# A decoder's second cross-attention: the order of the work behind its last item, and the banks that this work uses

## The chip, the core and the metric

The program runs on one core of one Trainium2 chip. A core has TensorE (PE: matmuls and transpositions, results to eight banks of PSUM), VectorE (DVE), ScalarE (ACT), GpSimd (POOL) and SyncE (SP), each with an instruction stream of its own, which runs in order; they wait for each other through semaphores. The metric is device time in microseconds for one execution, from the launch to the end of the last store. Smaller is better.

## What is computed

Two decoder layers; each is an attention, a cross-attention and a feed-forward part, with x = layernorm(x + part(x)) behind each. x is 8 items of 112 tokens by 256 values, the context 8 items of 375 by 192. The change lies in the second layer's cross-attention, whose stage also holds the last feed-forward part:

```python
def _L1_xattn_ref(x, context, Wq, Wk, Wv, Wo, bo):      # 8 heads of 128
    q = (x @ Wq).reshape(B, Tq, h, C) * SCALE
    k = (context @ Wk).reshape(B, Tk, h, C) * SCALE
    v = (context @ Wv).reshape(B, Tk, h, C)
    attn = jax.nn.softmax(jnp.einsum('bqhc,bkhc->bhqk', q, k), axis=-1)
    out = jnp.einsum('bhqk,bkhc->bqhc', attn, v).reshape(B, Tq, h * C)
    return out @ Wo + bo

def _L1_ffn_ref(x, base_w, base_b, lora_A, lora_B, router_w, router_b):
    result = jnp.einsum('bsd,od->bso', x, base_w) + base_b
    logits = jnp.einsum('bsd,ed->bse', x, router_w) + router_b
    gating = jax.nn.softmax(logits, axis=-1).astype(jnp.bfloat16)
    mid = jnp.einsum('bsd,dr->bsr', x, lora_A)
    lora_out = jnp.einsum('bsr,erd,bse->bsd', mid, lora_B, gating.astype(jnp.float32))
    return result + lora_out * SCALING
```

## The kernel before

The stages follow each other on the core: a state-space part, a cross-attention, a mixture of experts, a latent attention, and last `wide_cross_attention`, from about 727 us to the end of the profile. There the key and value weights are folded into the query and output weights, so scores are taken with the context itself, and the weighted context goes through `w_b`.

**Items and strips.** The loop runs over items i = 0 to 7 and over four strips u = 0 to 3 of two heads each. For a strip TensorE makes the scores of the next strip (`scores`, banks 1 and 2) and transposes the probabilities of this one (`turn`, banks 3 and 4). VectorE takes the maxima (`row_max`), copies the turned probabilities to SBUF (`copy_turned`) and scales the next ones (`normalize_heads`); ScalarE takes the exponentials (`exps`). For two strips, a half of an item, `weigh(i, half)` multiplies the turned probabilities with the context into banks 5, 6 and 7, called U_BANK: twelve matmul records for the first two, twelve for bank 7. `collect(i, half)` brings them back in two halves: ScalarE casts three tiles to fp32r (`ot_high`), VectorE subtracts the rest (`ot_low`). A `weigh` waits for the copies of its strips and for the `collect` before it. Half 1 of an item is weighed in the next item's strip 0; that of item 7 has no such place and stands behind the loop.

**Jobs.** All else of TensorE's work is a list of jobs with a number each: QUERY (queries of two items), CTX_REST and CTX_MAIN (transposing the context), OUT (output weights, 36 matmuls in fp32r), NT (transposing the normalized item), BASE (the feed-forward part's dense product with router and low-rank input), GATES (transposing the gated low-rank values) and LOW (their product with `lora_b`). `jobs(i, u, at)` says which job stands where in a strip (EARLY, MID, LATE), and `first_left` and `left` those behind the loop. All go through bank 0 (`JOB`): a job waits until `job_used` has counted every job before it, that is, until ScalarE (`drain`: QUERY, CTX, GATES, NT) or VectorE (`residual` for OUT, `base` for BASE, `add_low` for LOW) has emptied the bank. OUT also waits for both halves of `collect`, NT for `normalize`, GATES for `gates`.

**One item's way after its attention:** OUT, `residual` (add, statistics), `deviation` (ScalarE), `normalize`, NT, its copy to `xt`, BASE, `base` (small part, add, maximum), `gate_exps` (ScalarE), `gates`, GATES, its copy to `gm_t`, LOW, `add_low` (add, statistics), `end_deviation` (ScalarE), `finish`, store of the item by SyncE in the items' order. So several items are under way when the loop ends. Ahead of NT (7), TensorE runs eight products of the identity (`stream`), whose result nobody reads.

The order on each engine is the order in which these calls are written out. Line 1355 and 1358 are the scores, 1367 the turnings, 1382 the weighing's part in bank 7, 1306 and 1309 the context, 1319 GATES, 1321 LOW, 1324 NT; matmuls of line 101 are QUERY, OUT, BASE or weighing, told apart by their tiles.

## Time and profile before

| | us |
|---|---|
| timed runs, median of 3 | 997.63 (996.88 to 999.98) |
| profiled execution | 994.54 |
| its span, first to last instruction or packet | 992.7 |
| PE busy | 953.7 (96% of the span) |
| DVE busy | 587.3 (59%) |
| ACT busy | 414.3 (42%) |

A busy PE isn't PE at its peak, since matmuls are pipelined. The page's 40 slices show PE at nine or more tenths nearly throughout, and at 7 and 5 in the last two; the clock's row reads 9 (full) in all but the last, which reads 8. The chain that ended last consists of PE at the greatest part of its shares. Views used below are the timeline (instructions by start, merged, with the idle time of the engine before them), the chain, and tables of stretches with the granted clock, where 1.00 is the full 2.4 GHz and 0.50 is 1.2 GHz. A chain's piece lasts until the next one takes over, so it can be shorter than the same instruction in the timeline.

### The profile page before, as it was taken

Reading aid. Unit: us, or ns where it says so; the run is one execution under the profiler, and the core shown is the slowest. Engines: PE = TensorE matmul, PEld = TensorE weight load, DVE = VectorE, ACT = ScalarE, POOL = GpSimd, SP = SyncE. Lnnn points to the kernel's source line nnn. Section 1 sums busy time; section 2 is a strip of 40 time slices with the busy share of each in tenths; the row PEclk is TensorE's granted clock in tenths of the full one; section 3 lists DMA queues with packets and bytes.
Section 4 is the critical chain, followed back from the end, with each engine's and each line's share of the span. In section 5 each row is a group of like instructions: output and inputs, shape, how many; then the busy total and the mean of one; then the engine's idle time right before and its main releaser. Section 6 shows DMA issues by size and latency. Waiting matters only on the chain. (4 is left out here: it accounts for less than half of the span.)

```text
span 992.7 us, 17284 instructions
## 1 busy us (share of the span) xinstructions
PE 953.7 (96%) x6584; PEld 744.9 (75%) x6584; DVE 587.3 (59%) x1342; ACT 414.3 (42%) x1088; POOL 154.3 (16%) x151
## 2 busy tenths in 40 slices
PE   9899899999999999989999999999989999999975
PEld 4687777877878777768999998666657777767653
DVE  3788645555555565657756565368646454565554
ACT  3556534343343333436454545367643233232321
POOL 0333620110110100004443442300010000000000
PEclk9999999999999999999999999999999999999998
DMA  5500010000000000008511100720000000000000
GB/s 161 206 1 1 10 60 1 17 17 1 16 2 1 1 2 1 1 2 291 163 43 42 43 1 10 171 38 2 2 19 16 17 16 17 16 1 25 6 6 18
DMA packets 26825, 36.34 MB, mean 37 GB/s; under 512 B 3648, under 2 KB 22160, under 8 KB 26752
## 3 DMA queue, kind: packets, MB, share of 16 engines
q1 hardware_dynamic: 26752, 35.35, 12.1%
q8 instruction: 48, 0.79, 0.3%
q14 instruction: 25, 0.20, 0.1%
HBM read 30.75 MB, written 2.75 MB: 34 GB/s over the span
## 5 line engine op out<-in xcount | busy, mean ns | idle before, releaser
L1164 ACT ACTIVATE x_prob<-bank,x_negmax 112x375 f32<-112x375 f32 x128 | 72.2, 569 | 143.9 <-DVE x_negmax L1072 143.9
L1912 DVE TENSOR_TENSOR moe_h_low<-moe_sq,moe_h_high 128x512 fp32r<-128x512 f32 (+1 forms) x64 | 54.4, 871 | 50.6 <-ACT moe_h_high L2012 38.0
L1989 POOL TENSOR_TENSOR moe_sq<-moe_r 128x512 f32<-128x512 f32 (+1 forms) x64 | 64.2, 1006 | 102.8 <-ACT moe_r L2021 81.0
L1072 DVE TENSOR_REDUCE x_negmax<-bank 112x1 f32<-112x375 f32 x128 | 64.1, 542 | 9.5 <-PE bank L956 7.3
L2021 ACT ACTIVATE moe_r<-bank 128x512 f32<-128x512 f32 (+1 forms) x64 | 34.9, 545 | 72.6 <-PE bank L101 68.7
L101 PE MATMUL bank<-moe_w_low,moe_h_high 128*128 128x256 f32 x224 | 63.3, 283 | 0.0
L101 PE MATMUL bank<-moe_w_high,moe_h_low 128*128 128x256 f32 x224 | 63.3, 283 | 0.0
L101 PE MATMUL bank<-moe_w_high,moe_h_high 128*128 128x256 f32 x224 | 63.3, 283 | 0.0
L1077 DVE COPY x_prob_t<-bank 125x336 f32<-125x336 f32 x128 | 58.4, 497 | 2.9 <-PE bank L965 1.4
L956 PE MATMUL bank<-x_kt,x_qt 64*112 64x375 f32 x256 | 58.3, 521 | 1.2 <-issue 0.7
L1595 ACT ACTIVATE x_prob<-bank,x_negmax 112x375 f32<-112x375 f32 x64 | 36.1, 568 | 45.8 <-DVE x_negmax L1448 45.8
L965 PEld LDWEIGHTS bank<-const,x_prob 112*125 112x125 f32 x384 | 49.9, 188 | 6.6 <-issue 3.8
L965 PE MATMUL bank<-const,x_prob 112*125 112x112 f32 x384 | 52.8, 273 | 0.9 <-DVE x_prob_t L1077 0.8
L977 PEld LDWEIGHTS bank<-x_prob_t,x_v 125*64 125x64 f32 x768 | 37.0, 136 | 19.0 <-issue 15.2
L925 POOL COPY x_inv<-x_inv_head 112x512 f32<-112x512 f32 x16 | 9.8, 614 | 265.2 <-DVE x_inv_head L1083 265.2
L1604 ACT CAST x_ot_high<-bank 128x224 fp32r<-128x224 f32 x48 | 13.5, 354 | 81.9 <-PE bank L101 50.6
L977 PE MATMUL bank<-x_prob_t,x_v 125*64 125x112 f32 x768 | 45.4, 264 | 0.0
L101 PE MATMUL bank<-moe_xt_high,moe_w_high 128*128 128x384 f32 (+1 forms) x120 | 44.1, 367 | 1.0 <-DVE moe_w_low L1918 0.9
L1064 DVE COPY x_v<-bank 125x512 f32<-125x512 f32 x24 | 16.6, 691 | 45.4 <-PE bank L101 45.4
L101 PE MATMUL bank<-moe_xt_high,moe_w_low 128*128 128x384 f32 (+1 forms) x120 | 43.2, 360 | 0.0
L101 PE MATMUL bank<-moe_xt_low,moe_w_high 128*128 128x384 f32 (+1 forms) x120 | 43.2, 360 | 0.0
L101 PEld LDWEIGHTS bank<-moe_w_low,moe_h_high 128*128 128x128 f32 x224 | 42.9, 191 | 0.3
(377 smaller groups left out, 2365.5 us busy)
## 6 DMA issues: line engine op xcount, KB each, us to landing
moe_w<-in_L_ffn_W SPq DMA_DIRECT2D x15, 512.0 KB, 4.8
ctx_t<-in_ctx_t SPq DMA_DIRECT2D x8, 376.0 KB, 4.3
x_ctx_t<-in_ctx_t SPq DMA_DIRECT2D x8, 376.0 KB, 3.2
wk<-in_L_xattn_Wk SPq DMA_DIRECT2D x2, 1024.0 KB, 5.2
wv<-in_L_xattn_Wv SPq DMA_DIRECT2D x2, 1024.0 KB, 8.1
wq<-in_L_xattn_Wq SPq DMA_DIRECT2D x2, 1024.0 KB, 10.1
wo<-in_L_xattn_Wo SPq DMA_DIRECT2D x2, 1024.0 KB, 11.9
xt<-in_xt SPq DMA_DIRECT2D x1, 896.0 KB, 4.7
```

What stands on the lines that cost most here:

```text
L101: last = pe.matmul(out, lhs, rhs, start=(k == 0), stop=(k == len(pairs) - 1))
L956: last = pe.matmul(S_BANK(u, e)[0:T, 0:S], qt[i // 2 % 2][rows, u, i % 2 * T:(i % 2 + 1) * T], kt[p][rows, u, :], start=True, stop=True)
L965: last = pe.transpose(T_BANK(u, e)[0:SP_, k * T:(k + 1) * T], PROB(u, e)[:, k * SP_:(k + 1) * SP_], ident[0:T, 0:T])
L977: last = pe.matmul(bank[6 + u // HU][e * DH:(e + 1) * DH, at:at + T], v[p][:, k, g * DH:(g + 1) * DH], prob_t[u % 4][e][:, k, :], start=(k ...
L1064: return dve.tensor_copy(out, in_)
L1072: dve.tensor_reduce(negmax[:, g:g + 1], S_BANK(u, e)[0:T, 0:S], AX_X, ALU.max, negate=True).then_inc(max_ready, 1)
L1077: dve.tensor_copy(prob_t[u % 4][e][:, :, :], T_BANK(u, e)[0:SP_, 0:ST * T] .rearrange("s (k t) -> s k t", k=ST)).then_inc(pt_copied, 1)
L1164: act.activation(PROB(u, e)[:, :], S_BANK(u, e)[0:T, 0:S], ACT.Exp, bias=negmax[:, g:g + 1], accum_out=total[:, g:g + 1]).then_inc(p_ready, 1)
L1595: act.activation(prob[w % 2][e][:, :], S_BANK[e][0:T, 0:S], ACT.Exp, bias=negmax[:, g:g + 1], accum_out=total[:, g:g + 1]).then_inc(e_read ...
L1912: dve.tensor_tensor(h_low[half][:, m, 0:size], sq[m % 2][:, 0:size], h_high[half][:, m, 0:size].bitcast(F32), ALU.subtract).then_inc(low_d ...
L1989: pool.tensor_tensor(sq[m % 2][:, 0:size], r[m % 2][:, 0:size], r[m % 2][:, 0:size], ALU.mult).then_inc(sq_done, 1)
L2021: act.activation(r[m % 2][:, 0:size], bank[m][:, 0:size], ACT.Relu).then_inc(h_used, 1)
```

## The change

**At the stage's beginning** ScalarE empties QUERY (1, 0) ahead of the exponentials of strip 1, no longer behind them. (In the other items nothing changes.)

**Behind the last turning** TensorE weighs half 1 of item 7 at once, ahead of BASE (5) and NT (6). VectorE does `copy_turned(7, 3)` and `collect(7, 0)` inside `residual(6)`, right behind its add and ahead of its statistics. The weighing of half 1 signals each of banks 5 and 6 by `last_weighed`, bank 7 by `pv_done`; ScalarE casts each when it is there and signals it by `last_rounded`, and VectorE subtracts each in turn.

**The jobs of `left`** have banks of their own (`LEFT_BANK`, over all eight), a new order, and new waits (`last_job`): on the data that the job reads, and where a count of `left_vector` or `left_scalar` is needed, on that. They no longer wait for the job before. The idle products go into bank 7. The orders of VectorE and ScalarE behind the loop follow, and `base(7)` takes the maximum ahead of its add to x.

No instruction is added or removed, apart from semaphore operations.

```diff
     first_left = [(NT, B - 2)]
-    left = [(OUT, B - 1), (LOW, B - 4), (BASE, B - 2), (GATES, B - 3), (NT, B - 1), (BASE, B - 1), (LOW, B - 3), (GATES, B - 2),
+    left = [(LOW, B - 4), (OUT, B - 1), (GATES, B - 3), (BASE, B - 2), (LOW, B - 3), (NT, B - 1), (BASE, B - 1), (GATES, B - 2),
             (GATES, B - 1), (LOW, B - 2), (LOW, B - 1)]
+    LEFT_BANK = dict(zip(left, (2, 1, 3, 4, 6, 0, 5, 7, 3, 1, 2)))
+    left_on_vector = [job_ for job_ in left if job_[0] in (OUT, BASE, LOW)]
+    left_on_scalar = [job_ for job_ in left if job_[0] in (GATES, NT)]
...
             sem("pt_copied"), sem("pv_done"))
+        left_vector, left_scalar = sem("left_vector"), sem("left_scalar")
+        last_weighed, last_rounded = sem("last_weighed"), sem("last_rounded")
         ot_rounded, ot_split = sem("ot_rounded"), sem("ot_split")
...
                     for e in range(2):
-                        accumulate(pe, U_BANK[e][:, cols], [(c[:, k, 0:128], turned(e, k)) for k in range(ST)])
+                        last = accumulate(pe, U_BANK[e][:, cols], [(c[:, k, 0:128], turned(e, k)) for k in range(ST)])
+                        if i == B - 1 and half == 1:
+                            last.then_inc(last_weighed, 1)
                     for k in range(ST):
...
                             weigh(i, 0)
+                        if i == B - 1 and u == J - 1:
+                            weigh(i, 1)
                         for job_ in jobs(i, u, LATE):
...
                     job(job_)
-                weigh(B - 1, 1)
+
+                def last_job(job_):
+
+                    kind, i = job_
+                    if kind == LOW and i == B - 4:
+                        pe.wait_ge(job_used, number[(GATES, i)] + 1)
+                    elif kind == LOW:
+                        pe.wait_ge(left_scalar, left_on_scalar.index((GATES, i)) + 1)
+                    elif kind == OUT:
+                        pe.wait_ge(ot_split, 2 * B)
+                    elif kind == GATES:
+                        pe.wait_ge(gm_ready, i + 1)
+                    elif kind == BASE and i == B - 2:
+                        pe.wait_ge(job_used, number[(NT, i)] + 1)
+                    elif kind == BASE:
+                        pe.wait_ge(left_scalar, left_on_scalar.index((NT, i)) + 1)
+                    else:
+                        stream(pe, U_BANK[2], ident, 8)
+                        pe.wait_ge(normed_ready, i + 1)
+                    work(bank[LEFT_BANK[job_]], job_).then_inc(job_ready, 1)
+
                 for job_ in left:
-                    if job_ == (NT, B - 1):
-                        stream(pe, S_BANK[0], ident, 8)
-                    job(job_)
+                    last_job(job_)
...
                     cols, heads = slice(half * 2 * T, (half + 1) * 2 * T), slice(2 * half, 2 * half + 2)
-                    dve.wait_ge(ot_rounded, 2 * i + half + 1)
+                    last_half = i == B - 1 and half == 1
+                    if not last_half:
+                        dve.wait_ge(ot_rounded, 2 * i + half + 1)
                     for e in range(3):
+                        if last_half:
+                            dve.wait_ge(last_rounded, e + 1)
                         last = dve.tensor_tensor(ot_low[:, e, heads, :], U_BANK[e][:, cols].rearrange("d (j t) -> d j t", j=2),
...
+                def used(job_):
+
+                    if job_ in left_on_vector:
+                        return bank[LEFT_BANK[job_]], left_vector, left_on_vector.index(job_) + 1
+                    return JOB, job_used, number[job_] + 1
+
                 def residual(i):
+                    src, emptied, value = used((OUT, i))
                     chain.start(i)
-                    n = number[(OUT, i)]
-                    dve.wait_ge(job_ready, n + 1)
-                    dve.tensor_tensor(res[:, :], JOB[0:T, 0:D], core.x[:, i, :], ALU.add).then_inc(job_used, 1)
-                    dve.wait_ge(job_used, n + 1)
+                    dve.wait_ge(job_ready, number[(OUT, i)] + 1)
+                    dve.tensor_tensor(res[:, :], src[0:T, 0:D], core.x[:, i, :], ALU.add).then_inc(emptied, 1)
+                    if i == B - 2:
+                        copy_turned(B - 1, J - 1)
+                        collect(B - 1, 0)
+                    dve.wait_ge(emptied, value)
                     chain.link(dve.bn_stats(stats[:, :], res[:, :]))
...
-                    n = number[(BASE, i)]
-                    dve.wait_ge(job_ready, n + 1)
-                    dve.tensor_tensor(small[:, i, :], JOB[0:T, D:W], base_bias[:, D:W], ALU.add).then_inc(small_ready, 1)
-                    dve.tensor_tensor(core.x[:, i, :], JOB[0:T, 0:D], core.x[:, i, :], ALU.add).then_inc(job_used, 1)
+                    src, emptied, value = used((BASE, i))
+                    dve.wait_ge(job_ready, number[(BASE, i)] + 1)
+                    dve.tensor_tensor(small[:, i, :], src[0:T, D:W], base_bias[:, D:W], ALU.add).then_inc(small_ready, 1)
+                    if i < B - 1:
+                        dve.tensor_tensor(core.x[:, i, :], src[0:T, 0:D], core.x[:, i, :], ALU.add).then_inc(emptied, 1)
                     dve.wait_ge(small_ready, i + 1)
                     dve.tensor_reduce(top[:, i:i + 1], small[:, i, 0:E1], AX_X, ALU.max, negate=True).then_inc(top_ready, 1)
+                    if i == B - 1:
+                        dve.tensor_tensor(core.x[:, i, :], src[0:T, 0:D], core.x[:, i, :], ALU.add).then_inc(emptied, 1)
                     dve.tensor_scalar(mid2[:, i, :], small[:, i, E1:E1 + RK], 2.0, None, ALU.mult)
...
                 def add_low(i):
-                    n = number[(LOW, i)]
-                    dve.wait_ge(job_ready, n + 1)
-                    dve.tensor_tensor(core.x[:, i, :], JOB[0:T, 0:D], core.x[:, i, :], ALU.add).then_inc(job_used, 1)
-                    dve.wait_ge(job_used, n + 1)
+                    src, emptied, value = used((LOW, i))
+                    dve.wait_ge(job_ready, number[(LOW, i)] + 1)
+                    dve.tensor_tensor(core.x[:, i, :], src[0:T, 0:D], core.x[:, i, :], ALU.add).then_inc(emptied, 1)
+                    dve.wait_ge(emptied, value)
                     dve.bn_stats(end_stats[:, i, :], core.x[:, i, :]).then_inc(end_stats_ready, 1)
...
                             row_max(*after)
-                        copy_turned(i, u)
+                        if i < B - 1 or u < J - 1:
+                            copy_turned(i, u)
                         if u == 0 and i > 3:
...
                             residual(i - 1)
-                        if u == 2:
+                        if u == 2 and i < B - 1:
                             collect(i, 0)
+                        if i == B - 1 and u == J - 1:
+                            collect(i, 1)
                         if u == 3 and i > 1:
                             base(i - 2)
-                collect(B - 1, 1)
+                add_low(B - 4)
                 gates(B - 3)
                 residual(B - 1)
-                add_low(B - 4)
+                finish(B - 4)
+                normalize(B - 1)
                 base(B - 2)
-                normalize(B - 1)
-                finish(B - 4)
+                add_low(B - 3)
+                base(B - 1)
                 gates(B - 2)
-                base(B - 1)
-                add_low(B - 3)
                 gates(B - 1)
...
                     cols, heads = slice(half * 2 * T, (half + 1) * 2 * T), slice(2 * half, 2 * half + 2)
-                    act.wait_ge(pv_done, 2 * i + half + 1)
+                    last_half = i == B - 1 and half == 1
+                    if not last_half:
+                        act.wait_ge(pv_done, 2 * i + half + 1)
                     if i > 0 and half == 0:
...
                     for e in range(3):
+                        if last_half:
+                            act.wait_ge(*((last_weighed, e + 1) if e < 2 else (pv_done, 2 * B)))
                         last = act.copy(ot_high[:, e, heads, :], U_BANK[e][:, cols].rearrange("d (j t) -> d j t", j=2))
-                    last.then_inc(ot_rounded, 1)
+                        if last_half:
+                            last.then_inc(last_rounded, 1)
+                    if not last_half:
+                        last.then_inc(ot_rounded, 1)
...
                         after = following(i, u)
-                        if u == 2:
+                        if u == 2 or i == u == 0:
                             drain_all(jobs(i, u, EARLY))
...
                             exps(*after)
-                        if u != 2:
+                        if u != 2 and (i > 0 or u > 0):
                             drain_all(jobs(i, u, EARLY))
...
                         drain_all(jobs(i, u, LATE))
+                def drain_last(job_):
+                    act.wait_ge(job_ready, number[job_] + 1)
+                    empty(job_, bank[LEFT_BANK[job_]], copy).then_inc(left_scalar, 1)
+
+                collect(B - 1, 1)
                 drain_all(first_left)
                 gate_exps(B - 3)
-                collect(B - 1, 1)
+                end_deviation(B - 4)
+                drain_last((GATES, B - 3))
                 deviation(B - 1)
-                end_deviation(B - 4)
+                drain_last((NT, B - 1))
                 gate_exps(B - 2)
-                drain((GATES, B - 3))
-                drain((NT, B - 1))
+                end_deviation(B - 3)
                 gate_exps(B - 1)
-                end_deviation(B - 3)
-                drain((GATES, B - 2))
-                drain((GATES, B - 1))
+                drain_last((GATES, B - 2))
+                drain_last((GATES, B - 1))
                 end_deviation(B - 2)
                 end_deviation(B - 1)
-
```

**Where the instructions stand.** ScalarE at the beginning of the stage, from the table load of the stage on, before and after. Tiles are x1_prob (probabilities of a strip), x1_qt (queries), x1_w_b (output weights), x1_cn (context):

```order
L1632 ACT_TABLE_LOAD
L1595 ACTIVATE x1_prob0_0,x1_total<-bank1,x1_negmax 112x375
L1595 ACTIVATE x1_prob0_1,x1_total<-bank2,x1_negmax 112x375
L1595 ACTIVATE x1_prob1_0,x1_total<-bank1,x1_negmax 112x375
L1595 ACTIVATE x1_prob1_1,x1_total<-bank2,x1_negmax 112x375
L1587 COPY x1_qt1<-bank0 128x448
L1609 CAST x1_w_b_high<-x1_w_b 128x1024
L1587 COPY x1_cn1<-bank0 125x3x64
```

And after:

```order
L1684 ACT_TABLE_LOAD
L1640 ACTIVATE x1_prob0_0,x1_total<-bank1,x1_negmax 112x375
L1640 ACTIVATE x1_prob0_1,x1_total<-bank2,x1_negmax 112x375
L1632 COPY x1_qt1<-bank0 128x448
L1640 ACTIVATE x1_prob1_0,x1_total<-bank1,x1_negmax 112x375
L1640 ACTIVATE x1_prob1_1,x1_total<-bank2,x1_negmax 112x375
L1661 CAST x1_w_b_high<-x1_w_b 128x1024
L1632 COPY x1_cn1<-bank0 125x3x64
```

The copy of the queries from bank 0 has moved ahead of the exponentials of the next strip.

VectorE around the last turning, before and after, from the add of `residual(6)` on (x_pt are the turned probabilities):

```order
L1482 TENSOR_TENSOR x_res<-bank,x 112x256
L1484 BN_STATS x_stats<-x_res 112x6
L1485 MEMSET x_pad 112x1
L1486 BN_AGGR x_mv<-x_stats 112x2
L1487 TENSOR_SCALAR x_mv<-x_mv 112x1
L1469 TENSOR_TENSOR x_ot_low<-bank,x_ot_high 128x224 x3
L1453 COPY x_pt<-bank 125x3x112 x2
```

And after:

```order
L1519 TENSOR_TENSOR x_res<-bank,x 112x256
L1480 COPY x_pt<-bank 125x3x112 x2
L1500 TENSOR_TENSOR x_ot_low<-bank,x_ot_high 128x224 x3
L1524 BN_STATS x_stats<-x_res 112x6
L1525 MEMSET x_pad 112x1
L1526 BN_AGGR x_mv<-x_stats 112x2
L1527 TENSOR_SCALAR x_mv<-x_mv 112x1
```

The copies and the collection of half 0 have moved ahead of the statistics, and the collection behind the copies.

TensorE from the last turning on, before and after (lora_w is BASE, x_normed NT, x_pt the weighing, lora_b LOW; OUT (7) follows):

```order
L1367 MATMUL bank<-const,x_prob_0 125x112 x3
L1367 MATMUL bank<-const,x_prob_1 125x112 x3
L101 MATMUL bank<-lora_w,xt 112x272 x2
L1324 MATMUL bank<-const,x_normed 128x112 x2
L101 MATMUL bank<-x_pt,x_cn 128x224 x6
L1382 MATMUL bank<-x_pt,x_cn 64x224 x6
```

And after:

```order
L1372 MATMUL bank<-const,x_prob_0 125x112 x3
L1372 MATMUL bank<-const,x_prob_1 125x112 x3
L101 MATMUL bank<-x_pt,x_cn 128x224 x6
L1389 MATMUL bank<-x_pt,x_cn 64x224 x6
L101 MATMUL bank<-lora_w,xt 112x272 x2
L1329 MATMUL bank<-const,x_normed 128x112 x2
L1326 MATMUL bank<-lora_b,x_gm_t 112x256
```

The weighing has moved ahead of BASE and NT, and LOW (4) from behind OUT (7) to ahead of it.

TensorE behind OUT (7), before and after, with bank numbers:

```order
L1321 MATMUL bank0<-lora_b,x1_gm_t 112x256
L101 MATMUL bank0<-lora_w,xt 112x272 x2
L1319 MATMUL bank0<-const,x1_gm 64x112
L122 MATMUL bank1<-const 128x128 x8
L1324 MATMUL bank0<-const,x1_normed 128x112 x2
L101 MATMUL bank0<-lora_w,xt 112x272 x2
L1321 MATMUL bank0<-lora_b,x1_gm_t 112x256
L1319 MATMUL bank0<-const,x1_gm 64x112 x2
L1321 MATMUL bank0<-lora_b,x1_gm_t 112x256 x2
```

And after:

```order
L1324 MATMUL bank3<-const,x1_gm 64x112
L101 MATMUL bank4<-lora_w,xt 112x272 x2
L1326 MATMUL bank6<-lora_b,x1_gm_t 112x256
L122 MATMUL bank7<-const 128x128 x8
L1329 MATMUL bank0<-const,x1_normed 128x112 x2
L101 MATMUL bank5<-lora_w,xt 112x272 x2
L1324 MATMUL bank7<-const,x1_gm 64x112
L1324 MATMUL bank3<-const,x1_gm 64x112
L1326 MATMUL bank1<-lora_b,x1_gm_t 112x256
L1326 MATMUL bank2<-lora_b,x1_gm_t 112x256
```

LOW (5) stands ahead of the idle products now, and each job has a bank of its own in place of bank 0.

## Rows read from the trace of the kernel before

**Rows 1.** Stretches: us, busy (x count) of PE PEld DVE ACT POOL, clock, DMA.
```profile
958.00:968.00 10.00, 6.31 (x42) 4.84 (x40) 4.39 (x16) 2.44 (x11) 0.00 (x0) 1.00 0.00 1
...
981.00:993.00 12.00, 3.92 (x11) 1.27 (x9) 5.82 (x25) 1.99 (x10) 0.00 (x0) 0.70 0.10 29
```

**Rows 2.** Timeline, beginning of the stage: start us, us, engine, line, tiles, idle before.
```profile
729.36 1.78 PE L101 MATMUL bank<-xt,x_w_a 128*128 128x224 f32 x8
...
733.59 0.91 PE L1367 MATMUL bank<-const,x_prob 112*125 112x112 f32 x6
...
735.40 0.53 ACT L1587 COPY x_qt<-bank 128x448 f32<-128x448 f32 x1
...
735.98 0.54 PE L1309 MATMUL bank<-const,x_ctx_t 64*125 64x64 f32 x3 [1.49 <-ACT x_qt L1587]
```

**Rows 3.** Stretch of 4 us, PE alone: us, PE busy, clock, DMA share, GB/s.
```profile
736.00:740.00 4.00, 4.00 (x11) 0.57 0.00 0
```

**Rows 4.** Chain that ended last, beginning of the stage: start us, us, what.
```profile
735.51 0.43 ACT x_qt L1587
...
736.52 2.72 PE bank L1355 x4
...
739.24 1.18 PE bank L1358 x4
...
749.83 1.44 PE bank L1355 x4
...
751.28 0.82 PE bank L1358 x4
```

**Rows 5.** Timeline around the last turning.
```profile
958.67 0.42 DVE L1482 TENSOR_TENSOR x_res<-bank,x 112x256 f32<-112x256 f32 x1 [6.29 <-PE bank L101]
...
959.01 0.84 ACT L1604 CAST x_ot_high<-bank 128x224 fp32r<-128x224 f32 x3 [7.46 <-PE bank L101]
...
960.12 0.98 DVE L1469 TENSOR_TENSOR x_ot_low<-bank,x_ot_high 128x224 fp32r<-128x224 f32 x3
...
961.02 0.91 DVE L1453 COPY x_pt<-bank 125x336 f32<-125x336 f32 x2
...
963.41 0.41 PE L1324 MATMUL bank<-const,x_normed 112*128 112x112 f32 x2 [3.09 <-DVE x L1503]
```

**Rows 6.** Chain that ended last, from the last weighing on.
```profile
963.83 2.29 PE bank L101 x12
...
966.11 1.31 PE bank L1382 x12
...
969.45 4.46 PE bank L101 x36
...
977.92 1.80 PE bank L122 x16
...
979.95 0.35 ACT xt L1587
...
980.34 1.19 PE bank L101 x4
...
981.55 0.17 DVE x_small L1502
...
982.11 0.70 PE bank L1321 x2
...
984.87 0.27 PE bank L1319
...
988.19 0.43 DVE x L1521
...
989.99 0.41 DVE x L1532
```

**Rows 7.** Timeline, one item's gates on VectorE.
```profile
984.04 0.15 DVE L1510 RECIPROCAL x_gate_inv<-x_gate_sum 112x1 f32<-112x1 f32 x1
...
984.50 0.23 DVE L1515 TENSOR_TENSOR x_gm<-x_gate,x_mid 112x64 f32<-112x64 bf16 x1
```

## The prediction

> **What bounds the kernel now.** I read the table of stretches first [rows 1]. Until about 958 us TensorE hardly pauses. From 958 to 993 us it is 6.31 of 10 us busy, then 3.92 of 12: there the end is set by chains that pass from engine to engine. The change works on that tail and on one spot at the stage's beginning, so I read both in the timeline and the chain.
>
> The beginning [rows 2]: QUERY (1, 0) is complete in bank 0 at 729.36 + 1.78 = 731.14. ScalarE empties it at 735.40, behind the exponentials of strip 1. TensorE, whose next job needs bank 0, has finished turning at 733.59 + 0.91 = 734.50 and stands still until 735.98. Then, between 736 and 740 us, the granted clock reads 0.57 [rows 3], so mostly the 1.2 GHz level: the next scores take 2.72 and 1.18 us in the chain, against 1.44 and 0.82 for the same kind at 2.4 GHz [rows 4].
>
> The tail: after the last turning TensorE runs BASE (5) and waits for VectorE until 963.41 for NT (6), idle 3.09 us [rows 5], and only then does the last weighing. Behind it the chain goes weighing, three ScalarE casts, three VectorE subtractions, OUT (7) from 969.45 [rows 6]. After that every job takes bank 0 in turn, so jobs with their inputs ready wait until the one before has been emptied.
>
> **The change part by part.** I keep before's time axis and count the beginning separately. Forecast times are estimates from the rows named.
>
> *Beginning (ACT copies QUERY (1, 0) ahead of the second exponentials).* ScalarE's copy now falls at about 731.3, into its wait for VectorE's maxima, and costs nothing. The query of this job is used by item 2 only, nothing earlier. CTX_REST runs right behind the turning, 734.5 to 735.0, and the scores of strip 2 wait only for the exponentials, which end at 735.51 [rows 4]. They begin at 735.55 and not at 736.52: 0.97 us. With 0.55 us of idle time there in place of 1.49, I take the clock to stay up: 2.72 + 1.18 - 1.44 - 0.82 = 1.64 us more. The sum is 2.6 us. TensorE is the bound behind this (it is busy 4.00 of 4 us as soon as it runs again [rows 3], and hardly pauses until the tail), so the shift carries through. What is late next is the weight cast of 1 us that follows the exponentials on ScalarE; its VectorE half ends near 737.7, just ahead of the new maxima at 737.8, so it costs nothing.
>
> *The weighing first.* The residual of item 6 adds at 958.67 as before. Now the two copies of the last turning follow it (0.91), then the collection of item 7's first half (0.98) [rows 5]; the statistics go behind them. Add, copies and collection end near 961.0, and the weighing starts there, not at 963.83: 2.8 us. It ends at 961.0 + 2.29 + 1.31 = 964.6 [rows 6]. TensorE idles 1.7 us ahead of it. The delayed statistics push normalizing item 6 to about 962.3 to 963.3; NT (6) now needs it only at 966.4, so that cover holds with 3 us in hand.
>
> *Three signals.* Before, from the last weighing matmul to OUT (7) passed 969.45 - 967.42 = 2.03 us. Now the first two banks are cast and subtracted beside the third. Behind the last matmul stand one cast (0.35, the copy of the same shape at 979.95 [rows 6]) and one subtraction, a third of 0.98 plus its fixed part, which I take as 0.4. OUT (7) could start at 964.6 + 0.85 = 965.45. The split casts overlap less (0.84 for three together [rows 5], 3 x 0.35 apart), but the first two are hidden by 2.3 us of matmuls.
>
> *What stands ahead of OUT (7) now.* BASE (5), NT (6) and LOW (4) come between. BASE (5) takes 1.19 [rows 6], to 965.8; NT (6) shares bank 0 and waits for VectorE to empty it, about 0.55; NT (6) 0.34; LOW (4) about 0.6 (0.70 with its latency [rows 6]), into bank 2. OUT (7) starts at 967.3, against 969.45. So the jobs moved ahead eat 1.85 us of the signals' gain, and 2.15 us arrive. OUT (7) itself costs 4.46 [rows 6], and VectorE's residual adds at 971.8.
>
> *Eight banks.* Before, the 4.0 us between the end of OUT (7) at 973.91 and the eight idle products at 977.92 [rows 6] held LOW (4), BASE (6) and GATES (5), each waiting on VectorE. Now GATES (5) 0.2, BASE (6) 1.1 and LOW (5) 0.6 run back to back behind OUT (7), each in its own bank. The idle products start at 973.6 and last 1.80; normalizing item 7 (ready near 974.05) hides under them. ScalarE's copy of NT (7) moves from 979.95 to 973.6 + 2.03 = 975.65: the lead is 4.30 us, and BASE (7) is ready for VectorE at 977.25, against 981.55 [rows 6].
>
> *The last jobs.* From BASE (7) to GATES (7) passed 984.87 - 981.55 = 3.32 us [rows 6], with LOW (5) and its statistics between. Those are gone ahead. What stays is base (7), 0.72 (before, 0.56 passed from its first operation to the matmul it releases at 982.11 [rows 6]; the new order exposes one more wait), and two gate chains of 0.60 and, with the last operation's end, 0.69 (984.04 to 984.73 [rows 7]), with a handoff of 0.04: 2.05 us. That saves 1.27. From GATES (7) to the end of the last normalizing passed 989.99 + 0.41 - 984.87 = 5.53 [rows 6]. Now LOW (6) starts 0.2 behind GATES (7) (its input came earlier), takes 0.70, then add and statistics of item 6 1.21, then 989.99 - 988.19 = 1.80 from the last add to the last normalizing [rows 6], and 0.41: 4.36 with handoffs. The 1.21 is an estimate: the 1.80 less ScalarE's two steps of 0.2 with their handoffs. At 1.2 GHz, where these matmuls ran before (clock 0.50 and below 1 from 985 us, 0.70 for the whole stretch [rows 1]), LOW (6) takes 0.3 more: 4.66. I keep that value: 0.87 saved.
>
> Tail: 4.30 + 1.27 + 0.87 = 6.4 us; 6.7 with the clock up. The store behind it is unchanged.
>
> **The sum.** 2.6 + 6.4 = 9.0 us. Against the profiled execution: 994.54 - 9.0 = 985.5, its span 992.7 - 9.0 = 983.7. The three timed runs have a median of 997.63, 3.1 us above the profiled one; I carry the difference over to that: 988.6 us.
>
> One uncertain term is the clock. The trace shows a fall after 1.49 us of idle at 736 us [rows 2, 3], and none after 3.09 us at 963 us, where the stretch reads 1.00 [rows 1, 5]. So an idle time alone does not decide it. The Trainium skill ("TensorE: Matmul & The Clock Gate", Part 1: The HAM clock gate) says why that could be: the monitor runs freely, so the number of slow matmuls differs from run to run of one kernel. By that rule timed runs of before need not hold the fall of the profiled one, and the sum would be 7.4; by the trace alone it is 9.0. One profiled execution can't tell these apart.
>
> **The rivals.**
>
> *The clock's part of the beginning isn't gained.* Either it falls after all, with 0.55 us idle and turnings ahead, or the runs of before mostly lacked it. For it: the two idle times above. Then 0.97 + 6.4 = 7.4 us: 990.2.
>
> *A new fall in the tail.* TensorE now idles 1.7 us ahead of the weighing, directly behind turnings, as at 734.5. If the clock falls through the weighing or OUT (7), it costs what it did there, about 1.6 us: 990.2 too, and 991.9 with the first rival. Against it: the 3.09 us without a fall.
>
> *VectorE's order becomes the bound.* It is in order. The add of LOW (4) now stands ahead of the gates of item 5 and the residual of item 7; base (6) stands behind normalizing 7. If a wait there lasts 1 to 3 us longer than I sum, the gain is 4 to 6 us: about 992.5. Against it: each has over a microsecond of slack in the sum above except base (7) with the gates.
>
> *Slower than before.* The clock falls ahead of the weighing and doesn't come back, as the many short jobs keep TensorE half idle. Some 15 us of matmuls (weighing 3.6, OUT 4.4, idle products 1.8, the small jobs 5) at 2.72 / 1.44 = 1.9 times would cost 13 us, against 9.0: 1001.6. It decides from the point at which 10 us of these matmuls run slow. Against it: in the fall at 736 us, continuous work brought the clock back by 740 [rows 3].
>
> *The change doesn't do what it says*: OUT (7) still starts at 969 because the weighing waits on something not listed. Then only the banks' and the beginning's part, some 5 us: 992.6.
>
> **How the numbers follow.** Forecast (8 to 9.4 us saved) 0.52; clock's part at the beginning missing 0.20; a new fall in the tail 0.12; VectorE's order 0.09; not as it says 0.04; slower 0.03. The range takes in the first three and the spread of the timed runs, 996.88 to 999.98, about 1 us either way around a median: 986.8 to 992.0. A measurement of this kernel can tell about 0.3% from no change, 3 us. All cases but the slower one, and the ends of the fourth and fifth, save more: faster 0.94, same 0.03, slower 0.03.
>
> **What would show it right or wrong.** Right: a first copy of x_qt ahead of the second pair of exponentials, no idle time over 0.7 us ahead of the fourth scores, clock 1.00 from 736 to 740; the last weighing starting 1.8 us behind the last turning; OUT (7) starting 2.7 us behind its end, directly behind LOW (4); GATES, BASE and LOW behind OUT (7) without a VectorE wait; the last normalizing ending 16.7 us behind the start of OUT (7), where it was 21.0. Wrong: a granted clock under 1 between the weighing and the idle products; TensorE waiting for VectorE ahead of LOW (5); or a beginning shorter by 1 us only.

## The result, and the profile after

| | before | changed |
|---|---|---|
| median of the timed runs | 998.81 us (4 runs, 996.88 to 1001.05) | 985.62 us (4 runs, 985.38 to 987.15) |
| profiled execution | 994.54 us | 985.41 us |
| its span | 992.7 us | 983.6 us |

The ratio on record, changed over before, is 0.9871 with a 95% interval of 0.9844 to 0.9897; it is taken over all runs and isn't that of the medians, which is 0.9868. The change makes the kernel 13.2 us faster by the medians, but 9.1 us by the two profiled executions. The forecast was 988.6 us, range 986.8 to 992.0: the measured median lies under the range, 1.2 us below its lower end. The span forecast for the profiled execution was 983.7 us, and it measured 983.6.

The beginning of the stage, timeline of the changed kernel (start us, us, engine, line, tiles, idle before), against [rows 2]:

```profile
729.40 1.78 PE L101 MATMUL bank<-xt,x_w_a 128*128 128x224 f32 x8
...
731.22 0.53 ACT L1632 COPY x_qt<-bank 128x448 f32<-128x448 f32 x1
...
733.63 0.91 PE L1372 MATMUL bank<-const,x_prob 112*125 112x112 f32 x6
...
734.47 0.54 PE L1314 MATMUL bank<-const,x_ctx_t 64*125 64x64 f32 x3
...
735.61 1.51 PE L1360 MATMUL bank<-x_ctx_t,la_q_strips 128*112 128x375 f32 x4 [0.60 <-ACT x_prob L1640]
```

ScalarE empties the first queries at 731.22 in place of 735.40, the context's transposition follows the turning without a pause, and the idle time ahead of the scores is 0.60 us. The clock, in a table of stretches with PE alone as [rows 3], stays up where it read 0.57:

```profile
736.00:740.00 4.00, 4.00 (x21) 1.00 0.00 0
```

The chain of the changed kernel at that place, as [rows 4]: the scores last 1.51 and 0.82 us at 2.4 GHz, where they took 2.72 and 1.18.

```profile
735.61 1.51 PE bank L1360 x4
737.12 0.82 PE bank L1363 x4
737.94 1.71 PE bank L101 x8
```

The tail, timeline around the last turning, as [rows 5], and then the chain, as [rows 6]:

```profile
956.14 0.42 DVE L1519 TENSOR_TENSOR x_res<-bank,x 112x256 f32<-112x256 f32 x1 [6.29 <-PE bank L101]
...
956.49 0.91 DVE L1480 COPY x_pt<-bank 125x336 f32<-125x336 f32 x2
957.36 0.99 DVE L1500 TENSOR_TENSOR x_ot_low<-bank,x_ot_high 128x224 fp32r<-128x224 f32 x3
...
958.49 2.51 PE L101 MATMUL bank<-x_pt,x_cn 125*128 125x224 f32 x12 [1.74 <-DVE x_ot_low L1500]
...
962.71 0.39 DVE L1500 TENSOR_TENSOR x_ot_low<-bank,x_ot_high 128x224 fp32r<-128x224 f32 x1 [0.90 <-ACT x_ot_high L1653]
```

```profile
958.49 2.51 PE bank L101 x12
961.00 1.29 PE bank L1389 x12
...
965.01 4.43 PE bank L101 x36
...
971.06 1.98 PE bank L122 x16
...
973.27 0.35 ACT xt L1632
...
974.88 0.19 DVE x_small L1542
...
976.91 0.28 PE bank L1324
...
980.84 0.41 DVE x L1575
```

The copies and the collection follow the residual's add, the weighing starts 2.35 us behind it, the last subtraction ends at 963.10 (962.71 + 0.39), and OUT (7) starts only at 965.01. Behind OUT (7) nothing waits until the idle products end.

### The profile page after: what moved, and what is told of

Its sections match the earlier page's. It is cut to its first block and busy times, and to the rows that moved or that the text cites. A ratio compares the mean times of both kernels' runs of the same rounds, so it can differ in the third digit from the quotient of the medians.

```text
span 983.6 us, 17279 instructions
## 1 busy us (share of the span) xinstructions
PE 950.8 (97%) x6584; PEld 744.2 (76%) x6584; DVE 587.4 (60%) x1342; ACT 414.7 (42%) x1088; POOL 154.4 (16%) x151
```

## The experiments

Each ran in five rounds with runs of the kernel before beside it, apart from e12: e1 to e4 on one chip, e5 to e8 on another, e9 to e11 on a third, e13 to e15 on a fourth. There are 17 or 23 runs of before on a chip, twelve of e1, e2, e5, e6, e9 and e13, six of e3, e4, e7, e8, e10 and e11, and five of e14 and e15. Each run has a mean granted clock over its whole span; the last column but one is the mean of these. The ratios are taken over all runs as above, so they differ a little from those of the medians. In the cuts below, "..." marks lines left out, and comments that name a run are mine.

| | median us | before, same chip | difference | ratio, 95% interval | mean clock | edit |
|---|---|---|---|---|---|---|
| e1 | 999.38 | 999.51 | -0.1 | 1.0005, 0.9984 to 1.0025 | 0.9892 | none (before) |
| e2 | 994.18 | 999.51 | -5.3 | 0.9962, 0.9943 to 0.9981 | 0.9923 | beginning alone |
| e3 | 988.84 | 999.51 | -10.7 | 0.9895, 0.9872 to 0.9919 | 0.9937 | all but the beginning |
| e4 | 988.00 | 999.51 | -11.5 | 0.9882, 0.9858 to 0.9906 | 0.9943 | none (changed) |
| e5 | 995.50 | 997.90 | -2.4 | 0.9979, 0.9961 to 0.9996 | 0.9923 | before, idle products at the beginning |
| e6 | 995.18 | 997.90 | -2.7 | 0.9980, 0.9962 to 0.9998 | 0.9919 | before, idle products in the tail |
| e7 | 988.57 | 997.90 | -9.3 | 0.9908, 0.9881 to 0.9934 | 0.9930 | changed, one signal |
| e8 | 987.42 | 997.90 | -10.5 | 0.9897, 0.9868 to 0.9925 | 0.9917 | changed, no idle products |
| e9 | 994.14 | 998.05 | -3.9 | 0.9968, 0.9951 to 0.9984 | 0.9923 | before, weighing first alone |
| e10 | 983.60 | 998.05 | -14.5 | 0.9862, 0.9836 to 0.9889 | 0.9938 | new order |
| e11 | 985.04 | 998.05 | -13.0 | 0.9877, 0.9850 to 0.9903 | 0.9935 | new order, one signal |
| e13 | 994.62 | 998.67 | -4.1 | 0.9969, 0.9956 to 0.9983 | 0.9928 | before, idle products at both |
| e14 | 987.47 | 998.67 | -11.2 | 0.9897, 0.9876 to 0.9918 | 0.9942 | none (changed) |
| e15 | 982.80 | 998.67 | -15.9 | 0.9848, 0.9827 to 0.9870 | 0.9944 | new order |

### Why the medians part more than the traces: e1 and e4

Both kernels once more, unchanged.

> The kernel before, unchanged. Its profiled run was 994.54 us, its timed runs 996.88 to 1001.05, where the changed kernel's profiled run equals its timed ones (985.41 against 985.38 to 987.15). Theory A (clock luck: the timed runs of before hold more stretches at 1.2 GHz than its one profiled run): the trace taken here lies at 996 to 1000 us and shows granted clock under 1 in places where the first trace read 1.00, each worth 1 to 2 us. Theory B (something that no clock shows, a wait or a transfer that varies): times as wide as before, and stretches that are longer at full clock.

> The changed kernel, unchanged, beside the others on one chip. 985.4 to 987.2 us as before, and about 13 us under the median of the kernel before. Where single runs are above 986, the mean granted clock is lower (0.994 against 0.996), 1.7 us for each fall of about 3.4 us.

Single runs, each as time and mean granted clock:

```
before, e1:   992.40 0.997   994.99 0.993   997.30 0.991   998.08 0.989
              999.14 0.988   999.37 0.988   999.39 0.988  1000.58 0.988
             1000.66 0.988  1001.02 0.988  1001.88 0.986  1002.00 0.986
changed, e4:  984.67 0.997   985.78 0.996   987.97 0.994   988.03 0.994
              988.26 0.993   989.57 0.992
```

Time goes with the clock in both, by 0.9 to 1.0 us for each 0.001. That is theory A in its main part: the spread of a kernel's runs is time at 1.2 GHz. The changed kernel's runs reached further than the 985.4 to 987.2 us that I expected, and lie 11.5 us under before, not 13. The other half of theory A, that the trace taken here would be a long one, failed: it lies at 994.99 us and 0.993, as the first. But it shows that not every fall is tied to its place. Stretches of e1's trace, as [rows 3]:

```profile
444.00:448.00 4.00, 3.43 (x19) 0.90 0.61 208
448.00:452.00 4.00, 4.00 (x14) 0.67 1.04 312
712.00:716.00 4.00, 2.66 (x31) 1.00 0.00 0
716.00:720.00 4.00, 4.00 (x24) 1.00 0.01 2
736.00:740.00 4.00, 3.38 (x9) 0.67 0.00 0
740.00:744.00 4.00, 4.00 (x22) 0.91 0.00 0
```

The clock is at its lower level for a while around 448 us, in the mixture of experts, where the first trace read 1.00 throughout, and again around 738. Apart from its last microseconds, the first trace had two falls, at 14 and 738 us; the one at 14 us is missing in e1. The first trace's row:

```profile
12.00:16.00 4.00, 4.00 (x7) 0.61 0.52 122
```

So both traces hold two falls and both read 0.993 on average. One fall, added up over stretches of 2 us as (1 - clock) times length, comes to 1.68 to 1.72 us in every trace (those at the very end apart), which is 0.0017 of the span. The trace of e4 has a fall at 712 to 720 and, new to this kernel, one in the weighing, at 960 (PE idle 1.74 us just before it):

```profile
712.00:716.00 4.00, 3.03 (x17) 0.82 0.01 2
716.00:720.00 4.00, 4.00 (x17) 0.75 0.00 0
...
956.00:960.00 4.00, 2.26 (x18) 1.00 0.01 2
960.00:964.00 4.00, 4.00 (x17) 0.57 0.00 0
```

```profile
957.07 0.42 DVE x_res L1519
...
959.41 3.92 PE bank L101 x12
963.34 1.50 PE bank L1389 x12
...
967.56 4.40 PE bank L101 x36
```

The weighing's first part lasts 3.92 us in place of 2.51, and OUT (7) starts 10.49 us behind the residual's add (967.56 - 957.07), where it was 8.87 in the first trace of this kernel (965.01 - 956.14). So this fall costs 1.6 us. e3, e7 and e8 have it too; in e3 and e8 OUT (7) starts 10.54 and 10.50 us behind the add.

### Which place the median owes it to: e2 and e3, e5, e6 and e13

e2 is the kernel before with the beginning's part alone, e3 the changed kernel without it:

```diff
-                        if u == 2:
+                        if u == 2 or i == u == 0:
                             drain_all(jobs(i, u, EARLY))
...
-                        if u != 2:
+                        if u != 2 and (i > 0 or u > 0):
                             drain_all(jobs(i, u, EARLY))
```

> The kernel before with only the beginning's part of the change: the first queries emptied ahead of the second exponentials. By the prediction's sum 2.6 us faster than before where the clock fell at 736 us in the run of before, 1.0 where it did not. If the extra 4 us that the medians show belong to the beginning, the gain is 4 to 7 us and the spread over runs shrinks to about 2 us. If they belong to the tail, the gain is 1 to 2.6 us and the spread stays at 4 to 6 us.

> The changed kernel without the beginning's part: ScalarE empties the first queries behind the second exponentials, as before. By the prediction's sum 6.4 us faster than before. If the extra 4 us belong to the tail (its idle times of 3.1 and 2.0 us let the clock fall in most runs of before, and the new tail has none as long), the gain is 9 to 11 us with a small spread. If they belong to the beginning, the gain is 6 to 7 us and the spread stays wide.

Each part alone gains more than its share of the traces: 5.3 and 10.7 us by the medians (3.6 and 9.8 by the means, 998.43 to 994.85 and 988.62), against 2.6 and 6.4 forecast. e2's spread didn't shrink to 2 us: its runs lie between 992.43 and 998.61. The two parts add to more than both together, 16.0 against 11.5 by the medians and 13.4 against 11.0 by the means; the second excess, 2.3 us, is about twice its own standard error, so whether they really remove the same time in part stays open. At equal clock they do add up. A line through the 93 runs of before whose clock is on record falls by 0.87 us for each 0.001 of mean clock; e2 lies 1.1 us under it on average and e3 6.2, 7.3 together, against 7.0 for the changed kernel (15 runs, a line of the same slope) and 0.97 and 6.6 in the chains.

e5, e6 and e13 leave every wait and change nothing but what TensorE does in it:

```diff
                         turn(i, u)
+                        if i == u == 0:
+                            stream(pe, U_BANK[2], ident, 6)      # e5, e13
...
                 for job_ in first_left:
+                    stream(pe, S_BANK[0], ident, 12)             # e6, e13
                     job(job_)
                 weigh(B - 1, 1)
                 for job_ in left:
-                    if job_ == (NT, B - 1):
+                    if job_ in ((NT, B - 1), (OUT, B - 1)):      # e6, e13
                         stream(pe, S_BANK[0], ident, 8)
```

> The kernel before with six idle products of the identity (into bank 7, read by nobody) behind the first turning, where TensorE waits 1.49 us for bank 0. The wait itself stays; only the clock there is kept up. In the 35 runs of the kernel before so far, time goes with the mean granted clock, about 0.95 us for each 0.001, between 992.4 at 0.997 and 1002 at 0.986. If the falls that make the median are at the beginning, the median drops by 3 us or more and the mean clock from 0.989 to 0.992 or better. If they are in the tail or in other stages, it drops by 0 to 1.6 us.

> The kernel before with idle products in two waits of the tail: twelve ahead of NT (6), where TensorE waits 3.1 us, and eight ahead of OUT (7), where it waits 2.0 us. The waits stay, about 2.7 and 1.8 us of them are filled. If the clock falls in the tail in most runs of before, the median drops by 3 us or more and the mean clock rises to 0.992 or better. If the falls lie elsewhere, the time stays within 1 us of the kernel before.

> The kernel before with the idle products of both e5 and e6: six at the beginning, twelve and eight in two waits of the tail. All waits stay. If these two places hold all of the excess, the median is about 993 to 994 us, 4.5 to 5 us under the kernel before, with a mean clock of 0.994 to 0.995 and no run over 997. If other stages have a part, or if the two don't add up, it stays at 995 or above, as each alone.

With idle products at the beginning the median drops by 2.4 us and the mean clock rises from 0.9902 to 0.9923; in the tail by 2.7 us, to 0.9919; at both by 4.1 us, from 0.9898 to 0.9928. By the means it is 2.1, 2.3 and 3.2 us, and the intervals of e5 and e6 end just short of 1 (0.9996 and 0.9998). No work was saved, and e5 lies on the line of before (0.0 us off), so its gain is clock alone; e6 and e13 lie 0.6 and 0.8 us under the line, a remainder that the mean clock doesn't explain. Both thresholds of 3 us were missed, and the pair together missed 4.5 to 5 us: two places hold 4.1 of the 6.3 us by which the median of before (998.67) lies above its runs at 0.997 (992.24, 992.40 and 992.40). The rest lies elsewhere.

The traces differ on the two places. At the beginning all six that keep the wait of 1.49 us empty (before, e1, e3, e6, e9, e12) have a fall within 734 to 744 us, and none of the eleven others, where it is filled or gone, has one. That fall isn't luck, and by its size in the first trace (1.64 us) it is most of e5's gain. In the tail the traces of before (the first, e1 and e12) show no fall between 940 and 984 us, so the tail's part rests on the timed runs of e3 and e6 alone.

The trace of e5, with the beginning busy, shows other places: in the stage ahead, in the loop and in the tail:

```profile
712.00:716.00 4.00, 3.20 (x18) 0.82 0.01 2
716.00:720.00 4.00, 4.00 (x17) 0.76 0.00 0
736.00:740.00 4.00, 3.87 (x20) 1.00 0.00 0
...
944.00:948.00 4.00, 2.62 (x11) 0.83 0.00 0
948.00:952.00 4.00, 4.00 (x19) 0.74 0.10 29
...
960.00:964.00 4.00, 1.10 (x5) 0.96 0.01 2
964.00:968.00 4.00, 3.80 (x14) 0.61 0.00 0
```

> The kernel before, unchanged, one more profile. If its mean clock is 0.991 or less (the timed runs of before lie mostly at 0.988 to 0.991, its two traces at 0.993), the trace shows where the clock was at 1.2 GHz in such a run: by the reading that beginning and tail hold the falls, at 736 us and between 960 and 985 us; otherwise in other stages, as at 446 and 714 us in other traces.

e12 is one more profile of the kernel before. It came out at 994.57 us and 0.993, with falls at 446 and 736 us. So the profiled executions of before that I have, three, lie between 994.5 and 995.0, while its timed runs lie mostly at 0.988 to 0.991. At 0.0017 for a fall, an estimate from the traces, the timed runs of before (0.9894 to 0.9906 on average on the four chips) hold one and a half to two falls more than the two of each trace. I have no trace of a run at 0.988; where those falls are, and why the profiled ones keep to 0.993, stays open.

### The tail's parts: e9, e7 and e8

e9 is before with the weighing first, the three signals and VectorE's copies and collection moved, but the jobs in their old order through bank 0.

```diff
+                        if i == B - 1 and u == J - 1:
+                            weigh(i, 1)
                         for job_ in jobs(i, u, LATE):
                             job(job_)
                 for job_ in first_left:
                     job(job_)
-                weigh(B - 1, 1)
```

> The kernel before with the weighing's part alone: the last weighing at once behind the last turning, the copies and the collection ahead of item 6's statistics, signals in three parts. The jobs keep their order and bank 0, the beginning is as before. By the prediction's steps OUT (7) then starts behind NT (6) near 966.7 on the axis of before, where it was 969.45, and all behind it follows as before: 2.7 us at equal clock. If the banks are needed for the earlier weighing to count, it is 1 us or less.

Measured by the medians 3.9 us, of which part is clock (0.9906 to 0.9923). The trace has the chain's part:

```profile
959.98 0.42 DVE x_res L1490
...
967.81 0.42 PE bank L1325 x2
...
968.26 0.35 ACT xt L1600
...
968.66 4.49 PE bank L101 x36
```

OUT (7) starts 8.68 us behind the residual's add; in before it was 969.45 - 958.67 = 10.78 [rows 5, 6]. That is 2.1 us, not 2.7: through bank 0, OUT (7) has to wait until ScalarE has emptied NT (6), 0.35 and handoffs. From the add to the end of the last normalizing the trace takes 29.85 us, against 31.73 in before and 25.11 in the changed kernel: 1.9 us belong to the weighing's part, and the other 4.7 to the banks and the order together. No run parts those two.

e7 is the changed kernel with one signal for the weighing:

```diff
                     for e in range(2):
-                        last = accumulate(pe, U_BANK[e][:, cols], [(c[:, k, 0:128], turned(e, k)) for k in range(ST)])
-                        if i == B - 1 and half == 1:
-                            last.then_inc(last_weighed, 1)
+                        accumulate(pe, U_BANK[e][:, cols], [(c[:, k, 0:128], turned(e, k)) for k in range(ST)])
...
-                    if not last_half:
-                        act.wait_ge(pv_done, 2 * i + half + 1)
+                    act.wait_ge(pv_done, 2 * i + half + 1)
```

> The changed kernel without the signalling in three parts: ScalarE casts the last weighing's three banks when all are there, VectorE subtracts when all are cast. In the trace of the changed kernel the last subtraction ended at 963.10, and OUT (7) started only at 965.01, behind BASE (5), NT (6) and LOW (4). With one signal the subtractions would end at 962.3 + 0.85 + 1.0 = 964.2. By the prediction's reading, that the jobs ahead of OUT (7) hide the signals' gain, the time at equal clock stays within 0.3 us. If the signals carry part of the gain, it is 1 us slower.

The forecast of "within 0.3 us" failed. Its trace has the fall in the weighing as e4's, so the two compare:

```profile
956.87 0.42 DVE x_res L1513
...
965.69 0.99 DVE x_ot_low L1494 x3
...
966.76 0.34 DVE x L1538
...
967.14 0.41 PE bank L1329 x2
...
968.17 4.43 PE bank L101 x36
```

OUT (7) starts 11.30 us behind the residual's add, 0.8 us later than in e4. OUT (7) doesn't wait for the subtractions directly. They stand on VectorE ahead of base (5), base (5) releases NT (6), and NT (6) stands ahead of OUT (7). The runs at 0.993 and 0.994 agree: 988.3 to 989.2 against 987.2 to 988.3 for the changed kernel, on other chips. So the signals do pay, through the job behind them.

e8 leaves out the eight idle products ahead of NT (7):

```diff
-                        stream(pe, U_BANK[2], ident, 8)
                         pe.wait_ge(normed_ready, i + 1)
```

> The changed kernel without the eight idle products ahead of NT (7). In its trace they run from 971.06 to 973.04, and normalizing item 7 is done near 971.7, so they hold NT (7) up by 1.3 us. If the clock stays up without them, 1.3 us faster; if they are what keeps it up, the matmuls behind (BASE (7), LOW (6), LOW (7)) run at 1.2 GHz in more runs, which costs 0.3 to 1.5 us, and it is level or slower.

It is level with the changed kernel (10.5 us under before, against 11.2 and 11.5), and its mean clock, 0.9917, is the lowest of all kernels with the new tail. In its trace base (7) begins 9.17 us behind OUT (7)'s start in place of 9.87, but the clock falls already between 976 and 978 us, ahead of GATES (7), and the last normalizing ends 16.06 us behind OUT (7)'s start in place of 16.24. The idle products cost about what they save.

### A version that is faster than both: e10, e11 and e15

The order is planned from the rows above: BASE (5) and LOW (4) go into TensorE's wait ahead of the weighing, OUT (7) directly behind weighing and NT (6), LOW (6) ahead of GATES (7), without idle products; VectorE does base (5) ahead of normalizing item 6.

```diff
-    first_left = [(NT, B - 2)]
-    left = [(LOW, B - 4), (OUT, B - 1), (GATES, B - 3), (BASE, B - 2), (LOW, B - 3), (NT, B - 1), (BASE, B - 1), (GATES, B - 2),
-            (GATES, B - 1), (LOW, B - 2), (LOW, B - 1)]
+    first_left = [(LOW, B - 4), (NT, B - 2)]
+    left = [(OUT, B - 1), (GATES, B - 3), (BASE, B - 2), (LOW, B - 3), (NT, B - 1), (BASE, B - 1), (GATES, B - 2),
+            (LOW, B - 2), (GATES, B - 1), (LOW, B - 1)]
...
+                last_job((LOW, B - 4))
+                weigh(B - 1, 1)
```

> The changed kernel with another order of the jobs, meant to be faster: BASE (5) and LOW (4) stand in TensorE's wait of 1.74 us ahead of the last weighing, OUT (7) right behind weighing and NT (6), LOW (6) ahead of GATES (7), no idle products; VectorE's base (5) ahead of normalizing item 6. By the rows of the changed kernel OUT (7) starts 1.7 us earlier (963.3 in place of 965.0), the end of the last normalizing comes 3 to 3.7 us earlier: 981.5 to 982.5 us where the clock holds. If LOW (4) and BASE (5) ahead of the weighing only push it back, the gain is under 2 us. If the missing idle products cost clock, 1 to 1.5 us of it are lost.

> The kernel of the new order again, beside the changed kernel. By e10 it is 14.5 us under the kernel before, so 2 to 4 us under the changed kernel on the same chip, median 983 to 985 us. If e10 owed its time to its chip, it is within 1 us of the changed kernel.

> The changed kernel, unchanged, on one chip with e13 and e15: 985 to 990 us, median 986 to 988, 11 to 13 us under the kernel before.

Beside the changed kernel on one chip it is 4.7 us faster by the medians (982.80 against 987.47), more than the 2 to 4 expected, and every run of it is under every run of that. e10's median of 983.60 lies above the 981.5 to 982.5 that were expected with the clock up; its trace has falls at 448 and 946 us. e10's chain:

```profile
958.49 1.04 PE bank L101 x4
959.53 0.61 PE bank L1327 x2
...
960.22 2.51 PE bank L101 x12
...
964.89 4.52 PE bank L101 x36
...
979.63 0.41 DVE x L1576
```

OUT (7) starts 7.01 us behind the residual's add (957.88 in e10's timeline) in place of 8.87, and the last normalizing ends 15.15 us behind OUT (7)'s start in place of 16.24. The weighing starts 2.34 us behind the add, as without the two jobs: they fit into the wait, and TensorE is busy where it idled ahead of the weighing.

> The kernel of the new order without the signalling in three parts. Here only NT (6), 0.3 us, stands between the last weighing and OUT (7), so nothing hides the casts and subtractions: by the reading that the jobs hid the signals' gain in the changed kernel, this one is 1.0 us slower than the new order with three signals. If the signals gain nothing in themselves, it is level.

With one signal the new order is 1.4 us slower by the medians (985.04 against 983.60, one chip). In its trace OUT (7) starts 966.37 - 958.19 = 8.18 us behind the add, 1.17 later. The three signals are worth here what the prediction's step gave them, 2.03 - 0.85 = 1.18 us.

## Why the prediction was wrong, point by point

**The beginning: right.** The scores start at 735.61 and their chain ends at 737.94, forecast 735.55 and 737.81; before, 740.42 [rows 4]. The queries emptied there serve items 2 and 3, not item 2 only, but as the prediction says nothing earlier reads them.

**The weighing first: right.** It starts 2.35 us behind the residual's add, forecast 2.33 (961.0 - 958.67). Its two parts take 3.80 us, 0.2 more than taken.

**Three signals: right in size, wrong in what hides them.** The last subtraction ends 6.96 us behind the add (963.10 - 956.14), forecast 6.78. I wrote that the jobs ahead of OUT (7) eat the gain. e7 shows that without the signals base (5) comes later and OUT (7) with it, by 0.8 us.

**What stands ahead of OUT (7): right.** It starts 8.87 us behind the add, forecast 8.63.

**Eight banks and the last jobs: right.** NT (7) is copied 17.13 us behind the add (forecast 16.98), base (7) begins at 18.74 (18.58), GATES (7) follows in 2.03 us (2.05), the end in 4.34 us (4.66, or 4.36 with the clock up, which it was until past 976 us). The tail from the add to the end of the last normalizing went from 31.73 to 25.11 us: 6.6, forecast 6.4 to 6.7.

**The step that failed: "I carry the difference over to that".** The sum of 9.0 was right for the profiled executions, 9.1. I set it against a median whose runs hold more time at 1.2 GHz than the profiled one, and so took it, without a reason, that the change leaves that extra time in place. Runs of before lie between 992.24 us at 0.997 and 1002.29 at 0.986, around 998 to 999.5; the changed kernel's between 984.67 at 0.997 and 989.57 at 0.992. At the same clock, 0.997, the difference is 7.6 to 7.7 us, with one run of the changed kernel there, and over all runs, on lines of one slope, 7.0 us; the sum without its clock terms is 0.97 + 6.7. The whole span's mean counts the low clock of the last microseconds too, where TensorE has little left to do and which is shorter in the changed kernel, so this split is good to about 1 us. The other 3.5 to 6 us of the medians' 11.2 to 13.2 go with the clock: on its two further chips the mean clock rises by 0.0049 and 0.0044. The change removes long idle times at two places, and e5, e6 and e13 show what such places cost on average when little else changes, 2.4, 2.7 and together 4.1 us. The sum had 1.64 us for one fall at one place and none for the tail. The fall at the beginning was sized about right; the tail's part, put at nothing, is what the sum lacked, and in which instructions it lies stays open, as no trace of before shows it.

The Trainium skill ("TensorE: Matmul & The Clock Gate", Part 1: The HAM clock gate) says that the number of slow matmuls differs from run to run of one kernel. I used it for a gain that could be missing. The runs agree with it (0.986 to 0.997 for one kernel), but it works in both directions: a trace with one fall in the last stage may be a lucky one. The fall at the beginning was no case for it, as it came in six of six traces.

**The rivals.** The new fall in the tail came: four of the six traces of kernels with the new tail and old job order (e3, e4, e7, e8, not the first and not e14) have it in the weighing, at 1.6 us where I could size it. I gave it 0.12 on the ground that 3.09 us of idle had passed without a fall once. It didn't turn the result: in timed runs before loses more in its own tail (e3's mean clock is 0.9937 against 0.9894), though no trace of before shows that loss. So 0.12 was too low a chance for this fall, and 0.20 too high for missing the clock's part at the beginning, which was there in every trace that could show it and is 2.1 to 2.4 us by e5. The clock never stayed low through the tail, and nothing was slower than before. That the forecast of the profiled execution came within 0.1 us is in part luck: both profiled executions happened to hold the same fall at 14 us, which no step of the sum looked at.

## What to carry to other kernels

Before a difference of two traces is set against a median, compare the clock of the profiled run with that of the timed ones: a kernel whose runs spread over 10 us here held that spread in time at the lower clock, and removing an engine's wait is worth its length plus the falls that it causes on average over runs. Whether a fall belongs to its place or to the execution is seen from several traces: here one place had it in six of six. A wait that can't be removed can be filled: first with jobs that are ready (e10), else with idle products (e5, e6). A signal's value is read not only from who waits for its data, but from what stands behind the waiting instructions on their engine (e7).

## What the runs showed of the hardware

Apart from the last 5 to 11 us of every trace, the granted clock fell in the 17 traces only near 14, 448, 714, 738, 946 and 962 us. The fall near 738 us is in all six traces with an empty wait of 1.49 us there, and in none of the eleven without. The others came in some executions of a kernel and not in others: the traces of before have one at 14, 448 and 448 us, and the wait of 1.74 us ahead of the new kernels' weighing was followed by a fall in four of six. Near 448, 714, 738, 946 and 962 us TensorE had been idle for a part of the 4 us before; near 14 us it had not (4.00 of 4 us busy from 8 to 12). A fall cost 1.6 to 1.7 us where it could be sized (in the weighing and at the beginning). Runs of before lie around a line in their mean clock with a standard deviation of 0.5 us, the farthest 1.6 us off. Six idle products that filled a wait of 1.49 us cost no time that the runs show and gave back 2.4 us (e5).
